# Sorted tokens for the expert layer: one padded 128-row tile with one expert's weights in place of eight dense expert products

## The reference, cut to what matters

```python
xn = layernorm(x)                      # x: 16 batches x 512 tokens x 256
# attention, 16 heads of 64
q, k, v = split(xn @ wqkv.T)           # rmsnorm of q and k per head, rotary embedding
attn = softmax(causal(q @ k.T * scale)) ; a = (attn @ v) @ wo.T
# experts, 8 of them, 256 x 256 each
chosen = argmax(xn @ gate_w.T)         # one expert per token
f = xn + sum_e onehot(chosen)[e] * (xn @ expert_w[e].T)
out = x + a + f
```

## Time and profile before

| | us |
|---|---|
| median of 3 runs | 2467.36 |
| profiled execution | 2465.25 |
| its span | 2463.1 |
| TensorE busy | 2352.5 |
| VectorE busy | 1755.1 |
| ScalarE busy | 1450.9 |
| POOL busy | 1172.1 |
| TensorE clock granted, share of full | 0.997 |

### The profile page before, as it was taken

One profiled execution on the slowest core, in us unless ns is written; L12 is line 12 of the kernel. 1 busy time (PEld: TensorE's weight loads), 2 busy tenths in 40 slices (PEclk: granted clock), 3 DMA queues, 4 the chain that ended last, 5 costly groups with the idle time before them and its releaser, 6 DMA issues.

```text
span 2463.1 us, 49058 instructions
## 1 busy us (share of the span) xinstructions
PE 2352.5 (96%) x18048; PEld 1947.8 (79%) x18048; DVE 1755.1 (71%) x4009; ACT 1450.9 (59%) x4193; POOL 1172.1 (48%) x1822
## 2 busy tenths in 40 slices
PE   2999999999999999999999999999999999999998
PEld 1788788878888887887888888788878878888886
DVE  5677777777767777777777777767777776777775
ACT  1656566655665656665665666566556656655664
POOL 1554544455454445545544444554445445445442
PEclk9999999999999999999999999999999999999999
DMA  3000000000000000000000000000000000000000
GB/s 125 1 1 6 14 1 18 1 6 14 1 18 1 18 1 1 18 1 18 1 6 14 1 18 1 5 14 1 18 1 12 8 1 18 1 18 1 5 6 9
DMA packets 19596, 26.53 MB, mean 11 GB/s; under 512 B 1952, under 2 KB 18464, under 8 KB 18976
## 3 DMA queue, kind: packets, MB, share of 16 engines
q1 hardware_dynamic: 19360, 23.41, 3.0%
HBM read 15.02 MB, written 8.39 MB: 10 GB/s over the span
## 4 chain that ended last, share of the span: by engine, by line
PE 73%; DVE 16%; ACT 8%; issue 2%; DMA 1%; POOL 0%; SPq 0%; DVEq 0%
PE ps_g L419 34%; PE ps_s L476 13%; PE ps_o L502 12%; PE ps_p L491 8%; ACT prob L346 4%; PE ps_s L479 4%; DVE k_t L628 3%; DVE q_t L628 3%; DVE neg_max L634 3%; ACT k_t L340 2%; PE ps_g L510 2%; DVE o_n L645 1%; DVE ln_stat L573 1%; DVE xn L583 1%; DVE onehot L609 1%
## 5 line engine op out<-in xcount | busy, mean ns | idle before, releaser
L283 POOL TENSOR_TENSOR qk_rot<-qk_cos,qk_sin 128x128 f32<-128x128 f32 x1024 | 445.5, 456 | 1203.1 <-DVE qk_sin L620 1196.5
L346 ACT ACTIVATE prob<-ps_s,neg_max 128x256 f32<-128x256 f32 (+3 forms) x1024 | 530.8, 523 | 618.6 <-DVE neg_max L634 603.7
L419 PE MATMUL ps_g<-w_qkv,xn_t 128*128 128x384 f32 (+1 forms) x3072 | 604.3, 346 | 28.6 <-DVE xn_t L590 28.6
L419 PEld LDWEIGHTS ps_g<-w_qkv,xn_t 128*128 128x128 f32 x3072 | 529.2, 189 | 29.0 <-issue 29.0
L634 DVE TENSOR_REDUCE neg_max<-ps_s 128x2 f32<-128x512 f32 (+3 forms) x512 | 419.3, 819 | 119.9 <-PE ps_s L479 119.9
L620 DVE TENSOR_TENSOR qk_cos<-ps_g,t_cos 128x256 f32<-128x256 f32 x512 | 214.9, 420 | 352.6 <-ACT v L335 352.3
L353 ACT ACTIVATE prob_t<-ps_p 128x512 f32<-128x512 f32 (+3 forms) x512 | 361.8, 707 | 165.4 <-PE ps_p L491 165.4
L419 PE MATMUL ps_g<-w_exp,xn_t 128*128 128x256 f32 x3072 | 418.6, 285 | 19.7 <-DVE acc L658 17.7
L289 POOL TENSOR_TENSOR rms_inv<-ss,neg_half 128x8 f32<-128x8 f32 x256 | 421.6, 1647 | 0.0
L419 PEld LDWEIGHTS ps_g<-w_exp,xn_t 128*128 128x128 f32 x3072 | 381.2, 189 | 33.6 <-DVE acc L658 30.7
L476 PE MATMUL ps_s<-k_t,q_t 64*128 64x256 f32 (+3 forms) x3072 | 375.5, 349 | 28.3 <-DVE q_t L628 24.1
(11 more groups left out here) (62 smaller groups left out, 2204.9 us busy)
## 6 DMA issues: line engine op xcount, KB each, us to landing
xin<-in_x SPq DMA_DIRECT2D x16, 512.0 KB, 3.9
out<-acc SPq DMA_DIRECT2D x32, 256.0 KB, 2.1
prob_t<-in_expert_t SPq DMA_DIRECT2D x2, 1024.0 KB, 4.9
prob_t<-in_wqkv_t SPq DMA_DIRECT2D x2, 772.0 KB, 5.1
prob_t<-in_wqkv_t SPq DMA_DIRECT2D x2, 768.0 KB, 5.7
prob_t<-in_wo_t SPq DMA_DIRECT2D x1, 1024.0 KB, 4.7
t_cos<-in_rope_cos SPq DMA_DIRECT2D x1, 128.0 KB, 3.8
t_sin<-in_rope_sin SPq DMA_DIRECT2D x1, 128.0 KB, 3.9
```

The lines of the kernel that those rows point to most:

```text
L283: r = pool.tensor_tensor(rot[:, :, a, :], cos[:, :, a, :], sin[:, :, 1 - a, :], ALU.add)
L346: r = act.activation(prob[:, n % 2, h, 0:w], ps_s[:, h, 0:w], ACT.Exp, bias=neg_max[:, i, h:h + 1], scale=1.0, accum_out=row_sum[:, u % 2, ...
L419: r = pe.matmul(ps, lhs(a, c), rhs(b, c), start=(c == parts[0] and (a, b) == TERMS[0]), stop=(c == parts[-1] and (a, b) == TERMS[-1]))
```

## The change

Tokens of two batches (a group) are sorted by expert. Each expert's tokens are padded to whole tiles of 128 rows; 8 tiles + 7 are always enough, so a group has NS = 15 tiles, some of them zeros. The steps of group g, whose batches are 2g and 2g + 1:

- `choose` also keeps a bf16 one-hot. In pair 0 of the odd batch TensorE counts ranks (nine bf16 matmuls), and VectorE takes them.
- One unit later `find_slots` works out each token's row and each tile's expert: 13 small dependent instructions on VectorE. Then POOL scatters the group's eight xn tiles to DRAM with eight indirect DMAs.
- From the second unit after that, one tile is done per unit: SyncE fetches its rows and, by an expert number that it reads from SBUF, its split weights (512 KB); TensorE transposes the rows (2) and multiplies (6 matmuls); ScalarE and VectorE take the transposed rows; ScalarE takes the result; SyncE stores it to DRAM. In the last group three tiles are done per unit, in the last five units.
- When a group's tiles are done, POOL gathers each batch's rows back with four indirect DMAs, VectorE adds them to acc one unit later, and SyncE stores the batch in one DMA.

Around it: w_exp is no longer in SBUF; VectorE splits one expert's weights and one slice of w_out in each of the first eight units (`split_weights`, four instructions), and SyncE stores the former to DRAM. values run in two steps; transpose_inverse and take_inverse come later; project is last in TensorE's unit, after transpose_qk, and take_projection early in VectorE's next unit. In pair 6 the transposes of xn come after those of q and k. acc has four buffers, xn two, xn_t one.

The diff, cut to its core:

```diff
+    G = B // GROUP            # GROUP = 2
+    GT = GROUP * NT
+    NS = GT + E - 1
-        w_exp = sb("w_exp", [P, 2, NC, E, C], F32R)
+        w_tile = sb("w_tile", [P, 2, 2, NC, C], F32R)
+        w_dram = nc.dram_tensor("w_dram", [E, P, 2, NC, C], F32).ap()
+        x_dram = [nc.dram_tensor(f"x_dram{n}", [NS * P, C], F32).ap() for n in range(2)]
+        y_dram = [nc.dram_tensor(f"y_dram{n}", [NS * P, C], F32).ap() for n in range(2)]
...
+        def sorted_tiles(u):
...
+                    if u == (U - 5 + s // 3 if g == G - 1 else g * GROUP * PAIRS + 11 + s):
+                        found.append(g * NS + s)
...
+            def fetch(i):                                    # SyncE
+                g, s = divmod(i, NS)
+                if i >= 2:
+                    sp.wait_ge(s_xs_t, i - 1)
+                    sp.wait_ge(s_expert, i - 1)
+                sp.wait_ge(s_scattered, 16 * GT * (g + 1))
+                sp.dma_start(x_rows_s[:, i % 2, :], x_dram[g % 2][s * P:(s + 1) * P, :]).then_inc(s_xs_loaded[i % 2], 16)
...
+                e = sp.value_load(tile_expert_i[0:1, g % 2, s:s + 1], min_val=0, max_val=E - 1)
+                sp.dma_start(w_tile[...], w_dram[bass.ds(e, 1), ...]).then_inc(s_w_tile[i % 2], 16)
...
+                for i in sorted_tiles(u):
+                    store(i)
+                    if i + 2 < G * NS:
+                        fetch(i + 2)
...
+            def scatter_rows(g):                             # POOL, at the end of its unit
+                pool.wait_ge(s_slots, g + 1)
...
+                for t in range(GT):
+                    pool.indirect_dma_start(x_dram[g % 2], bass.IndirectOffsetOnAxis(ap=slot_i[:, g % 2, t:t + 1], axis=0),
+                                            xn[:, t // NT, t % NT, :], None).then_inc(s_scattered, 16)
+            def gather_rows(b):
...
+                if b >= 1:
+                    pool.wait_ge(s_y_added, b)
+                for t in range(NT):
...
+                    pool.indirect_dma_start(y_back[:, t, :], None, y_dram[g % 2],
+                                            bass.IndirectOffsetOnAxis(ap=at, axis=0)).then_inc(s_y_back, 16)
...
                 if live(u + 1):                              # ScalarE
                     take_qkv(u + 1, 3)
+                for i in tiles[0:2]:
+                    take_xs(u, i)
+                if live(u):
+                    softmax(u, 2)
                 if live(u - 1):
                     take_inverse(u - 1)
-                if live(u):
-                    softmax(u, 2)
+                if live(u):
                     take_pt(u, 1)
                 if live(u - 1):
                     take_o(u - 1)
+                for i in tiles[0:1]:
+                    take_ys(u, i)
+                for i in tiles[2:3]:
+                    take_xs(u, i)
+                for i in tiles[1:2]:
+                    take_ys(u, i)
...
                 if live(u):                                  # TensorE
                     scores(u, 1)
                 if live(u - 1):
-                    values(u - 1)
+                    values(u - 1, (0, 1))
...
-                if live(u - 1):
-                    transpose_inverse(u - 1)
+                for i in tiles[0:2]:
+                    transpose_xs(u, i)
                 if live(u):
                     scores(u, 2)
                     transpose_probs(u, 1)
-                if projection(u):
-                    project(u)
-                if live(u):
-                    experts(u, (0, 1))
+                if live(u - 1):
+                    values(u - 1, (2, 3))
+                    transpose_inverse(u - 1)
+                for i in tiles[0:1]:
+                    expert(u, i)
+                for i in tiles[2:3]:
+                    transpose_xs(u, i)
+                for i in tiles[1:2]:
+                    expert(u, i)
                 if live(u):
                     scores(u, 3)
                     transpose_probs(u, 2)
+                for i in tiles[2:3]:
+                    expert(u, i)
                 if live(u + 1):
                     transpose_qk(u + 1)
+                if turns_x(u):
+                    transpose_xn(batch_of(u) + 1)
+                if ranks_in(u) is not None:
+                    ranks(u)
+                if projection(u):
+                    project(u)
-                if live(u):
-                    experts(u, (2, 3))
...
+                if projection(u - 1):                        # VectorE, after row_max(u, 0)
+                    take_projection(u - 1)
-                    take_experts(u - 1, (2, 3))
...
                     rope_products(u + 1, 3)
+                for i in tiles[0:2]:
+                    take_xs(u, i)
...
+                if slots_in(u) is not None:                  # after normalise_o, before row_max(u, 3)
+                    find_slots(slots_in(u))
...
+                if 0 <= u < E:                               # at the end of the unit, after take_o
+                    split_weights(u)
+                if added_in(u) is not None:
+                    add_experts(added_in(u))
```

More of the change, by code:

```diff
@@ L1 @@
 from contextlib import ExitStack
+from functools import lru_cache
 import numpy as np
@@ new lines, in sorted_tiles, with back_in @@
+        @lru_cache(None)
+        def sorted_tiles(u):
+            found = []
+            for g in range(G):
+                for s in range(NS):
+                    if u == (U - 5 + s // 3 if g == G - 1 else g * GROUP * PAIRS + 11 + s):
+                        found.append(g * NS + s)
+            return tuple(found)
+        def back_in(u):
+            for b in range(B):
+                g, half = divmod(b, GROUP)
+                if u == (U + half if g == G - 1 else g * GROUP * PAIRS + 27 + half):
+                    return b
+            return None
@@ new lines, in added_in, with projection, uses @@
+        def added_in(u):
+            if u == U + 3:
+                return B - 1
+            b = back_in(u - 1)
+            return None if b == B - 1 else b
+        def projection(u):
+            if not 3 <= u < U + 3:
+                return None
+            return divmod(u - 3, 2)
+        @lru_cache(None)
+        def uses(u):
+            found = []
+            if live(u + 1):
+                found += ["qkv0", "qkv1", "qkv2", "qkv3"]
+            tiles = sorted_tiles(u)
+            found += [f"xs{i}" for i in tiles[0:2]]
+            if live(u - 1):
+                found += ["inv"]
+            found += [f"ex{i}" for i in tiles[0:1]] + [f"xs{i}" for i in tiles[2:3]] + [f"ex{i}" for i in tiles[1:3]]
+            if live(u + 1):
+                found += ["kt", "qt"]
+            if turns_x(u):
+                found += ["xt0", "xt1"]
+            if ranks_in(u) is not None:
+                found += ["rank"]
+            if projection(u):
+                found += ["proj"]
+            return tuple(found)
@@ L204, in xt_bank, with tile_unit, loads @@
             return g_bank((b - 1) * PAIRS + XT_PAIR, f"xt{c}") if b else c
-        def expert_bank(u, t):
-            return g_bank(u, f"experts{t // 2}")
-        def projection(u):
-            if not 3 <= u < U + 3:
-                return None
-            group, half = divmod(u - 3, 2)
-            return group, half, g_bank(u, "proj")
+        def tile_unit(i):
+            return next(u for u in units if i in sorted_tiles(u))
+        def loads(i):
+            return 16 * (i // 2 + 1)
         chunk = 2 * P * NT * 2
@@ L254, in _ @@
+            for u in units:
+                unit(u)
+            for n in range(2):
+                sp.wait_ge(s_out_stored[n], 16 * B // 2)
         @block.gpsimd
@@ L309, in unit @@
                     row_deviations(batch_of(u) + 1)
+                if slots_in(u) is not None:
+                    scatter_rows(slots_in(u))
+                if back_in(u) is not None:
+                    gather_rows(back_in(u))
             row_deviations(0)
@@ L436, in qkv, with transpose_xs @@
                 n = NT * u + t
[L437 removed]
+                product(bank(qkv_bank(u, t), (s_products, n + 1))[:, 0:gate + 3 * PW], lambda a, c: xn_t[:, a, c, tile(t)],
                         lambda w, c: w_qkv[:, w, c, at:at + gate + 3 * PW], range(NC)).then_inc(s_qkv, 1)
[L440 to L447 removed]
+            def transpose_xs(u, i):
+                pe.wait_ge(s_xs_loaded[i % 2], loads(i))
+                ps = bank(g_bank(u, f"xs{i}"), (s_xs_lo, i + 1))
+                for c in range(NC):
+                    r = pe.transpose(ps[:, tile(c)], x_rows_s[:, i % 2, tile(c)], ident[:, :])
+                r.then_inc(s_xs_t, 1)
@@ new lines, in expert, with ranks @@
+            def expert(u, i):
+                pe.wait_ge(s_xs_lo, i + 1)
+                pe.wait_ge(s_w_tile[i % 2], loads(i))
+                product(bank(g_bank(u, f"ex{i}"), (s_ys, i + 1))[:, 0:C], lambda a, c: x_cols_s[:, i % 2, a, c, :],
```

(15 more changed lines are left out.)

293 lines of the change are left out of this document (217 added, 76 removed).

## The result

The changed kernel takes **2620.27 us** (median of 4 runs, 2619.64 to 2620.86), the kernel before 2467.09 beside it: ratio 1.0623, 95% interval 1.0604 to 1.0641, slower. Forecast 2560, range 2468 to 2650; the narrower range of the forecast's own mechanism, 2510 to 2620, ends where the measured time lies. The profiled execution took 2620.86 (span 2618.8), 155.6 above that of before; the sum had +96. The sign, the place and the mechanism held, and 60 us were missing.

The account below looks back on a forecast made before the run. The softmax chain through ScalarE and VectorE, not TensorE, was taken as the bound. Terms -16 + 21 + 56 - 14 + 10 + 28 + 11 = +96 on 2465.25 gave 2561, stated as 2560 us; range 2468 to 2650.

Parts of the forecast that it names:

- steps of once a batch: Choose, row_stats, normalise_x, take_xt, start_rows: 5.2 us a batch instead of 3.8, +21 us in all (ends 0 and +45).
- first eight units: split_weights at the end of VectorE's unit, about 1.65 us each with 0.4 of slack: +10 us.
- ranks, find_slots: Per group: nine rank matmuls before project, 0.8 us; 13 dependent VectorE steps ahead of row_max(3), 2.4 us.
- scatter unit: Eight indirect DMAs on POOL at 1.1 us each delay rotate(0), so VectorE's third rope_products is 1.5 us late.
- gathers and adds: Per group: the second gather on POOL 1.1 us, the first nothing, add_experts at VectorE's unit end 1.5 us.
- three-tile units: Four units near the end wait for the third tile's rows with two buffers: +7 us each, +28 (ends +10 and +50).
- tail: After the last unit's first scores: last y store, two gathers, adds, final store, 41 us against 29.8, +11 (ends +5 and +25).
- The chain: The softmax chain through ScalarE and VectorE, not TensorE, sets each unit: 18.16 us with a tile, 17.82 without.
- Steps of once a group: Ranks, find_slots, scatter, gathers and add_experts: 7.3 us per two-batch group, +56 us in all (ends +30 and +110).
- the price of the low end: Rival 3: the chain holds but additions are at their low ends, POOL at 0.46: 2475 to 2510 us; 15 in 100.
- the second rival: POOL's queue bounds around each scatter and gather: 2646 us at 2.0 us per indirect DMA, about 2775 at 3; 17 in 100.
- a clock below full in mid-run: TensorE's new waits could lower its clock in mid-run, making the prediction wrong on the slow side; no size given.

Follow-up runs that it names:

- Experiment 2: The changed kernel with each tile's expert product issued twice into the same bank: 2623.05 us, ratio 1.0632.
- experiment 3: The changed kernel with transpose_inverse and take_inverse back before softmax(2) and values(2, 3) ahead of transpose_probs(1): 2534.13 us, ratio 1.0269.
- experiment 1: The kernel before without its expert matmuls and take_experts (experts' part of the output missing): 2499.66 us, ratio 1.013.
- Experiment 4: The changed kernel with scatter and gather as plain DMAs on SyncE's queue instead of POOL's, rows unsorted: 2560.43 us, ratio 1.0376.
- experiment 8: The changed kernel with three buffers instead of two for the tile's rows and weights, fetched three tiles ahead: 2586.23 us, ratio 1.0482.
- experiment 12: The changed kernel plus unread matmuls, 12 per unit without a tile and 6 in five units around each group's steps: 2619.09 us, ratio 1.0619.
- experiment 5: The kernel before without experts, plus 12 unread matmuls in each unit behind transpose_qk: 2420.84 us, ratio 0.9812.
- experiment 11: The kernel before with choose, row_stats, normalise_x and start_rows moved on VectorE behind row_max(1): 2436.79 us, ratio 0.9875.
- run 33: Not a label: words of "made a run 33 us longer", which tells of experiment 1, the kernel before without experts, 2499.66 us.

## Why the prediction was right, and what it had too small

| term | forecast | measured in the changed kernel |
|---|---|---|
| ordinary unit | 18.16 | 18.13 |
| steps of once a batch, above ordinary | 5.2 | 5.3 (0.78 + 1.33 + 0.70 + 2.44) |
| start | -14 | -13.8 |
| first eight units, all terms | +9.7 | +14.5 |
| ranks, find_slots, per group | 0.8 + 2.4 | 0 + 3.5 |
| scatter unit above ordinary | 1.5 | 3.3 to 5.2, mean 4.1 |
| gathers and adds, per group | 2.6 | 5.2 to 6.8, mean 5.7 |
| three-tile units, four | +28 | +39 |
| tail | +11 | +14.7 |

**The chain: right.** The view that decided was the window of the early unit: 12 matmuls less had saved 0.78 and no more. Experiment 2 shows the room on TensorE, experiment 3 gives back the 0.48 of take_inverse to the hundredth, and experiment 1's 17.51 is the 17.47 that was called the floor.

**The steps of once a batch and the start: right**, by the rows of the same kernel.

**The step that was mis-sized: "Steps of once a group".** Eight find_slots units, eight of the scatter and six pairs of gathers take 95 us above ordinary ones where 53 stood in the sum: +41. POOL's lateness is about 30 of them, by the units below. VectorE's third rope_products waits for rotate(0), as the prediction has it, and the trace shows how late that is, here in that later unit of the scatter:

```profile
1192.92 1.70 POOL L445 TENSOR_TENSOR qk_rot<-qk_cos,qk_sin 128x128 f32<-128x128 f32 x4
...
1193.90 0.42 DVE L917 TENSOR_TENSOR qk_cos<-ps_g,t_cos 128x256 f32<-128x256 f32 x1 [2.32 <-POOL qk_rot L445]
```

In seven of the eight scatter units it starts 9.4 to 9.6 us behind the unit's q_t low part, right behind POOL's rotate, and in an ordinary unit 5.8: 3.6 late where the sum has 1.5. The unit has no tile and takes 17.8 without that; with it, 21.4. Eight DMAs are 10.1 us and not 8.8, one of them is 0.5 longer still, and each tenth counts once POOL is late. In the eighth, the unit of 21.99 above, the third rope_products starts another 0.6 later, for ScalarE's third qk_sq came 1.7 us behind its product; why stays open. TensorE's slow start in these units isn't on this path: the third rope_products starts at the same place whether the third product was done 5.0 or 6.5 us into the unit. What is on the chain is a later fall of the clock, behind a second wait of TensorE. Two scatter units, the one just shown and one with such a later fall:

```profile
1185.21:1206.63 21.42, 17.32 (x118) 13.47 (x118) 11.08 (x24) 10.99 (x32) 15.17 (x20) 0.92 0.34 111
871.58:894.03 22.45, 18.85 (x118) 14.49 (x118) 11.05 (x24) 11.10 (x32) 15.31 (x20) 0.85 0.34 106
```

The unit of the scatter is 21.4 without that fall and that of the second gather 22.1; what the eight and the six have above these is 6 and 3 us. Experiment 4 divides the gathers: without POOL's DMAs the unit of the first is 1.3 shorter, where nothing stood in the sum, and that of the second 2.5 at full clock, where 1.1 stood; the two adds are 1.4 (1.5 forecast). find_slots and ranks come out near the sum by luck: ranks cost nothing where 0.8 stood, and find_slots 3.5 where 2.4 stood, since the 0.6 that ScalarE was to hide and more was on the chain. Of the rivals, the price of the low end (POOL at 0.46 an instruction) and that of the high end (2.0) are out: the value lay near the nearest rows. But the place that the second rival named, POOL's queue around each scatter and gather, is where most of the missing time is; at 3 us for each DMA its own terms make about 2740, not 2775.

**The three-tile units (+11) and the tail (+4)** were right in mechanism, the rows' DMA with two buffers, as experiment 8 shows: it takes away TensorE's wait of 5.58 us. In the unit shown there TensorE gets the third tile's rows 18.6 us in, where the prediction's steps make 18.0. Part of the 11 belongs to another term: the unit of 31.0 also holds the second gather of the seventh group, priced under the group's steps. Behind the wait TensorE is at the lower clock, 35 us in the four units and 3 in experiment 8; the two effects weren't separated.

**The first eight units (+5)** are the clock: with it full from the second unit on, experiment 12 takes 157.1. The traces of experiments 2 and 4, with the same code in these units, have 160.4 and 160.5, and 26 us at the lower clock where this one has 35. The prediction named a clock below full in mid-run as its danger on the slow side; it came. Its price is 5 us here and, as an estimate from the units above with and without a later fall, 9 in those of scatter and gathers: some 14 of the 60, with the three-tile units left out. 41 + 5 + 11 + 4 = 61, within 1 us of what was missing.

**A theory that fell.** After experiments 1 and 5 the lower clock looked like the answer to a good part of the 60 us, and the expectation of experiment 12 says so. Time at the lower level isn't time lost: at the start of the scatter's unit the chain waits for POOL, and TensorE's slow matmuls lie beside it.

## What to carry to other kernels

Before taking work off the busiest engine, look in the profile for a unit that already lacks some of that work: its length is what the change can reach, and the chain of waits in it names what must be shortened first. Price each new step at the place in its engine's queue where it will stand: the same sort was 6% slower than the dense kernel with its steps ahead of what others waited for, and 2.4% faster with them in gaps, halved and fetched a tile sooner, with the inverse back in its gap. When a step's own clean-up helps the kernel before as well, measure it there too, or the change is credited with another's gain: of the 2.4%, 1.2% stand against the dense kernel of experiment 11.

## What the runs showed of the hardware that was not expected

- Taking 3072 matmuls out made a run 33 us longer, and putting 1536 unread ones back made it 79 us shorter (experiments 1 and 5). After waits of 2.5 to 3.1 us TensorE's matmuls ran at the lower of its two levels, 5.6 us for 18 in place of 3.4.
- What the lower level costs depends on who waits: 79 us of run time for 177 us less at it there; 1.2 us in a scatter unit of experiment 4, where VectorE waits for TensorE's products, and nothing for the same fall in the changed kernel, where it waits for POOL.
- An indirect DMA of 128 rows of 1 KB holds POOL for 0.96 us and 0.30 to the next one, scatter and gather alike; some take up to 1.45, mostly beside VectorE's low part of o_t.
